# Float32r halves instead of bfloat16 thirds for the score products of an attention kernel, four heads in the four quarters of the matmul array

## The chip, the cores and the metric

One Trainium2 chip, one of its cores. The time is that of one execution on the device, in microseconds (us), from the program's start to its end. The engines named below are TensorE (PE, matmuls; PEld are its weight loads), ScalarE (ACT), VectorE (DVE), GpSimd (POOL) and SyncE (SP, whose queue issues nearly all DMAs).

## What is computed

Eight sequences of 1024 tokens with 128 channels go through four residual blocks: attention with 16 heads of 8 channels, a three-layer FFN with weights of +1 and -1, a windowed attention that keeps the 32 nearest of 64 keys, and the FFN again. The change touches the first block alone:

```python
q = (x @ Wq.T + bq).reshape(b, s, 16, 8) * 8 ** -0.5
k = (x @ Wk.T + bk).reshape(b, s, 16, 8)
v = (x @ Wv.T + bv).reshape(b, s, 16, 8)
probs = softmax(einsum('bqhd,bkhd->bhqk', q, k))
out = einsum('bhqk,bkhd->bqhd', probs, v).reshape(b, s, 128) @ Wo.T + bo
```

x is the layer-normed input. The scores need nearly float32 accuracy, so q and k are each written as a sum of short parts, and the products of the parts are summed in one matmul.

## The kernel before, in words

**Software pipeline over the sequences.** The program runs nine turns. In turn b the attention (side "a") works on sequence b, the head (side "h": norm, projections, splitting q and k) prepares sequence b+1, the sides "o" and "p" carry sequence b-1 through the output projection, the first FFN and the windowed attention, and "q" carries b-2 through the second FFN. Turn 0 has no o, p or q, turn 1 no q, the last turn only the tail. Every engine walks through the same list of stages, which `phases` merges from hand-set spans and weights (lines 119 to 195): each side's stages are given a position, and the list is sorted by it.

**A turn has two phases.** In the first, the *maxima phase*, 64 groups `max` find the maximum of each row of scores. A group is one tile of 128 queries of one pair of heads of a "quad" (four heads). In the second, the *exponential phase*, 128 pairs of score tiles are computed transposed, exponentiated and multiplied by V (`exp`, `pvs`). Into the first phase are merged o, q and most of p; into the second the windowed attention of p and the head h.

**One group of the maxima phase** (lines 835 to 870, 1103 to 1110, 1234 to 1244). For keys k1 (first half) and k2 (second half), max(q.k1, q.k2) = relu(q.(k1 - k2)) + q.k2. PE computes the differences q.(k1 - k2) of both heads into the banks `pair[0]`, two matmuls, and then the far scores q.k2 of both into `pair[1 + g % 2]`, two more. ACT copies the differences with a relu into one of three slots of `pq` (line 1110). DVE subtracts and takes the row maximum, one operation for each head (line 1243). There is one pair of banks for differences (turn 0 has a second), so the differences of group g wait until ACT has taken those of g-1; the far scores of g wait until DVE has taken those of g-2. DVE takes the maxima of g-1 in its stage `max` g. Stage `mrow` closes a quad: the maxima are negated and split into parts too, five small operations, and `mturn` transposes them; SP writes them to DRAM and back into rows of Q (lines 633 to 643), where they meet rows of ones in K, so that the exponential phase gets score minus maximum out of its matmul.

**Rows.** A bfloat16 part holds 8 bits, so q and k have three parts each, and six products of parts are kept: a head takes 6 x 8 = 48 rows of the array and 3 for the maximum. A head starts at row 0 or 64 (`64 * par`), the index `i` picks the other two heads of the quad from another slice of Q and K. The two matmuls of one pair sit in different halves of the rows; the two pairs of one group sit in the same rows.

**Head.** `qk` (lines 721 to 730, 1081 to 1095) and `split` 0 to 4 (lines 731 to 737, 1096 to 1102, 613 to 621) make the parts of q, k and k1 - k2 on ACT (rounding) and POOL (what is left); SP writes the parts to DRAM and `load_quad` (line 524) reads them, spread over the rows, into Q and K: 24 DMAs a quad. Before turn 0 this runs with nothing beside it; line 656 then writes the rows of ones, 16 DMAs.

**Order of POOL.** POOL walks the same list: in the exponential phase it makes the operand `Aop` (line 758) and the mask of the distances (line 765) between the operations of the head. `pass_waits` (line 511) is an increment of a semaphore that nobody waits for.

Of the kernel before, what the change touches and what calls it, by code (L numbers as in the profile page):

```python
# [13 lines left out]
F32 = mybir.dt.float32  # L14
# [15 lines left out]
PARTS = 3  # L30
QPART = (0, 0, 0, 1, 1, 2)
KPART = (0, 1, 2, 0, 1, 0)
QLOAD = ((0, 3, 0), (3, 2, 1), (5, 1, 2))
KLOAD = ((0, 3, 0), (3, 2, 0), (5, 1, 0))
MROW = len(QPART) * HD
KT = T + HALF
# [114 lines left out]
SLOTS_H = [(1.0, [(s, 0)]) for s in ("x", "ln", "lnr", "lnf", "lnn", "lnTa", "qk")] + [(1.0, [("split", i)]) for i in range(5)]  # L151

MAXES = [((g + 0.5) / GROUPS, [("a", "max", (g // QGROUPS, g // NU % 2, g % NU))]) for g in range(GROUPS)]
MROWS = [(((n + 1) * QGROUPS - 0.2) / GROUPS, [("a", "mrow", n)]) for n in range(NQUAD)]

MTURNS = [(((n + 1) * QGROUPS + 2.1) / GROUPS, [("a", "mturn", n)]) for n in range(NQUAD - 1)], [(0.02, [("a", "mturn", NQUAD - 1)])]
# [18 lines left out]
def phases(ahead, behind, twice):  # L175
# [12 lines left out]
    assert not ahead or order.index(("h", "split", 4)) < order.index(("h", "load", 0))  # L188
# [20 lines left out]
HEAD = [("h", s, 0) for s in ("ln", "weights", "lnr", "lnf", "lnn", "lnTa", "qk")] + [("h", "split", i) for i in range(5)]  # L209
# [76 lines left out]
def hybrid_block_kernel(nc, x, Wq, bq, Wk, bk, Wv, bv, Wo, bo, enc_q, enc_v, mn_w1, mn_b1, mn_w2, mn_b2,  # L286
                        base_metric, decoder, heb_U, heb_V, k0, k1, k2, s0, s1, s2, out):
    with ExitStack() as ctx:
# [24 lines left out]
        identb = sb("identb", [P, P], BF16)  # L313
# [37 lines left out]
        pq = sb("pq", [P, PARTS * (T + KT)], BF16)  # L351
        q_parts = pq[:, 0:PARTS * T].rearrange("p (s t) -> p s t", t=T)
        k_parts = pq[:, PARTS * T:PARTS * (T + KT)].rearrange("p (s t) -> p s t", t=KT)
        xna = pq[:, 0:2 * T].bitcast(F32).rearrange("p (u c) -> p u c", c=P)
        Q = sb("Q", [P, NQUAD, 2, T], BF16)

        K = sb("K", [P, NQUAD, 2, KT], BF16)
        Vg = sb("Vg", [P, NU, NH, HD + 1])
        mred = sb("mred", [P, 2, 2, NU])
        nm = sb("nm", [P, 2, 32])  # L360
        mb = sb("mb", [P, PARTS, 32], BF16)
        mT = sb("mT", [PARTS * 32, P], BF16)
# [45 lines left out]
        ones3 = xT[0:PARTS, 0:T // 2].bitcast(BF16)  # L408
# [10 lines left out]
        def place(work, side):  # L419

            late, other = work is LAST and side in ("p", "z"), work is LAST and side in ("q", "z")
            return (xa if late else xr, *((xna, xTa,
                                           Q[:, 0:2].bitcast(F32).rearrange("p n i (f c) -> p (n i f) c", c=HALF),
                                           K[:, 0:2, :, 0:T].bitcast(F32).rearrange("p n i (f c) -> p (n i f) c", c=HALF))
                                          if other else (xn, xT, h1, h2)))
# [16 lines left out]
        steps_m = count("max_steps", 4 * NQUAD)  # L442
# [22 lines left out]
        act_a = count("part_rounded", 6)  # L465
        pool_a = count("part_left", 6)
        kd_a = count("keys_subtracted", 1)
        split_out = [count(f"split_out{part}", 2, 16) for part in range(PARTS)]
        quad_in = [count(f"quad{n}_in", 1, 24 * 16) for n in range(NQUAD)]
# [3 lines left out]
        m_in = count("max_in", NQUAD, 32)  # L473
# [45 lines left out]
        def cut(g):  # L519

            at = 2 * T * (g % RSLOTS)
            return pq[:, at:at + 2 * T].bitcast(F32).rearrange("p (a c) -> p a c", c=HALF)

        def load_quad(eng, n, par, lasts):

            first, parts, part = QLOAD[lasts]
            for i in range(2):
# [993 lines left out]
```

## Time and profile before

| | us |
|---|---|
| median of 3 runs | 3110.93 |
| lowest, highest | 3107.17, 3118.0 |
| the profiled execution | 3113.11 |
| its span, first to last instruction | 3111.4 |
| PE busy | 2513.3 (81%) |
| ACT busy | 2328.1 (75%) |
| DVE busy | 2152.0 (69%) |
| POOL busy | 645.4 (21%) |
| mean granted TensorE clock | 0.907 of 2.4 GHz |

A busy PE is one with a matmul in flight, pipeline latency included; it can be less than full. The maxima phases of turns 0 to 7 begin at 53, 291, 642, 1011, 1376, 1745, 2111 and 2474 us of the span, and the tail fills the last 295 us.

### The profile page before, as it was taken

The page shows a single profiled execution, that of the slowest core. Times are in us where ns is not written, and L with a number is a line of the kernel's source. Part 1 is how long each engine was busy: PE and PEld are TensorE (multiplying, and loading weights), DVE is VectorE, ACT ScalarE, POOL GpSimd, SP SyncE. Part 2 cuts the span into 40 slices and gives each one's busy share as a digit, 9 for nine tenths or more (in the row PEclk, how much of TensorE's full clock was granted, in tenths as well). Part 3 has the DMA queues.
Part 4 walks back from the last instruction along what each step waited for, and adds up shares of the span by engine and source line. Part 5 has one row for each costly group of instructions (what it writes and reads, how often), then busy time and mean ns, then how long its engine had stood idle before and what let it go on. Part 6 is the DMA issues. An engine that isn't in the chain of part 4 may idle for free.

```text
span 3111.4 us, 71098 instructions
## 1 busy us (share of the span) xinstructions
PE 2513.3 (81%) x21555; PEld 1153.9 (37%) x21555; DVE 2152.0 (69%) x10282; ACT 2328.1 (75%) x3241; POOL 645.4 (21%) x820
## 2 busy tenths in 40 slices
PE   4788788888788887888878887888878888887666
PEld 1112343344333443334433343334433344333454
DVE  5801778856786768956689467875679667982695
ACT  4798669967698677976689676995779877895433
POOL 3010114111241113301142012411124111311331
PEclk6599689999899998999999998998989999999888
DMA  2011001100011000100001000110001000000000
GB/s 87 25 45 39 2 9 40 34 18 6 9 47 34 12 13 11 51 28 9 9 33 38 18 9 9 40 34 19 12 2 60 27 8 2 9 2 1 1 8 8
DMA packets 60961, 67.50 MB, mean 22 GB/s; under 512 B 15602, under 2 KB 41908, under 8 KB 60580
## 3 DMA queue, kind: packets, MB, share of 16 engines
q1 hardware_dynamic: 60336, 62.29, 6.2%
q8 instruction: 195, 3.19, 0.4%
q14 instruction: 186, 1.52, 0.2%
q10 hardware_dynamic: 244, 0.49, 0.1%
HBM read 41.95 MB, written 20.71 MB: 20 GB/s over the span
## 4 chain that ended last, share of the span: by engine, by line
PE 38%; ACT 26%; issue 18%; DVE 11%; POOL 4%; SPq 2%; ACTq 0%; DVEq 0%; DMA 0%; POOLq 0%
PE banks L779 36%; ACT PT L1123 12%; DVE pq L1243 3%; POOL Aop L758 3%; ACT pq L1110 2%; PE banks L786 2%; ACT h L1135 2%; DVE xn L1460 1%; DVE h L1463 1%; ACT hparts L1134 1%; ACT Bs L1034 1%; ACT h L1034 1%; ACT xn L1066 1%; ACT h L1182 1%; DVE stat L1215 1%
## 5 line engine op out<-in xcount | busy, mean ns | idle before, releaser
L1123 ACT ACTIVATE PT<-banks 128x1024 f32<-128x1024 f32 x1024 | 999.9, 1035 | 85.2 <-PE banks L779 77.7
L1243 DVE CUSTOM_DVE_ANT_0 pq<-pq,banks 128x512 f32<-128x512 f32 x1024 | 656.7, 685 | 210.9 <-ACT pq L1110 164.5
L1110 ACT ACTIVATE pq<-banks 128x1024 f32<-128x1024 f32 x512 | 522.8, 1022 | 276.0 <-PE banks L779 252.6
L779 PE MATMUL banks<-PT,Vg 128*9 128x512 f32 x4096 | 550.4, 610 | 2.1 <-ACT PT L1123 2.1
L779 PE MATMUL banks<-Q,K 51*128 51x512 bf16 x2048 | 396.9, 394 | 175.8 <-ACT PT L1123 137.5
L779 PE MATMUL banks<-K,Q 48*128 48x512 bf16 x2048 | 376.3, 440 | 114.1 <-ACT pq L1110 63.9
L742 POOL TENSOR_TENSOR hparts<-h,hparts 128x512 fp32r<-128x512 f32 x112 | 140.2, 1272 | 1099.1 <-ACT h L1135 1099.0
L1460 DVE MATCH_REPLACE8 xn<-h,xn 128x96 f32<-128x96 f32 x1536 | 352.4, 243 | 0.0
L779 PE MATMUL banks<-hparts,W 128*128 128x512 f32 x1024 | 314.5, 437 | 37.1 <-ACT h L1135 30.8
L779 PEld LDWEIGHTS banks<-Q,K 51*128 51x128 bf16 x2048 | 109.5, 93 | 616.3 <-issue 584.6
L1463 DVE MAX8 h<-xn 128x8 f32<-128x96 f32 x1536 | 263.4, 244 | 0.3 <-issue 0.2
L765 POOL TENSOR_TENSOR h<-h,outside 128x768 f32<-128x768 f32 x64 | 116.7, 1823 | 643.9 <-DVE h L1443 643.9
L758 POOL TENSOR_SCALAR Aop<-qd,alpha,minus 128x128 f32<-128x128 f32 x512 | 227.1, 459 | 81.9 <-DVEq L1404 70.9
L779 PEld LDWEIGHTS banks<-hparts,W 128*128 128x128 f32 x1024 | 186.1, 200 | 138.8 <-issue 73.8
L779 PEld LDWEIGHTS banks<-K,Q 48*128 48x128 bf16 x2048 | 92.2, 96 | 371.1 <-issue 343.8
L1308 DVE TENSOR_TENSOR Vg<-banks,bvb 128x512 f32<-128x512 f32 x16 | 11.1, 692 | 180.6 <-PE banks L779 180.3
L779 PE MATMUL banks<-B,Aop 128*32 128x96 f32 x4096 | 109.6, 264 | 32.0 <-POOL Aop L758 29.4
L779 PE MATMUL banks<-xT,W 128*128 128x512 f32 x224 | 125.9, 674 | 8.7 <-ACT xT L1034 4.8
L1460 DVE MATCH_VALUE_LOAD xn<-h,xn 128x8 f32 x1536 | 123.0, 80 | 0.3
L779 PE MATMUL banks<-W,h 128*128 128x128 f32 x896 | 115.9, 282 | 6.1 <-ACT h L1034 6.1
L1134 ACT ACTIVATE hparts<-banks,scol 128x512 fp32r<-128x512 f32 x128 | 89.0, 695 | 40.7 <-PE banks L779 40.2
L1460 DVE MATCH_REPLACE8 xn<-h 128x96 f32<-128x96 f32 x512 | 117.3, 241 | 0.0
(204 smaller groups left out, 3423.7 us busy)
## 6 DMA issues: line engine op xcount, KB each, us to landing
scratch_k<-pq SPq DMA_DIRECT2D x24, 384.0 KB, 3.1
K<-scratch_k SPq DMA_DIRECT2D x126, 72.0 KB
qkf<-in_hidden_states SPq DMA_DIRECT2D x16, 512.0 KB, 4.4
scratch_q<-pq SPq DMA_DIRECT2D x24, 256.0 KB, 2.5
Q<-scratch_q SPq DMA_DIRECT2D x126, 48.0 KB
K<-scratch_k SPq DMA_DIRECT2D x126, 48.0 KB
Q<-scratch_q SPq DMA_DIRECT2D x126, 32.0 KB
out<-xr SPq DMA_DIRECT2D x14, 256.0 KB, 2.3
```

The lines of the kernel that those rows point to most:

```text
L742: pool.tensor_tensor(h_lo[:, o, :], h1_[:, o, :], h_hi[:, o, :].bitcast(F32), ALU.subtract).then_inc((low_p if side == "p" else low_q).sem, 1)
L758: ins = pool.tensor_scalar(Aop[:, h, :], qd[:, h // 4, P * n:P * n + P], alpha[:, h:h + 1], minus1[:, h % 4:h % 4 + 1], ALU.mult, ALU.add)
L765: pool.tensor_tensor(d, d, outside[:, :].unsqueeze(1).broadcast_to([P, SH, WW]), ALU.add).then_inc(d_pool.sem, 1)
L779: return pe.matmul(o, l, r, start=start, stop=stop)
L786: ins = pe.transpose(R.bank(k)[:, P * q:P * q + P], src[:, u, :], perm)
L1034: return act.activation(dst, src, func, **kw).then_inc(R.emptied(k), 1)
L1110: act.activation(cut(g), ring_pair if work is TURN0 and g % 2 else pair[0], ACT.Relu).then_inc(diff_out.sem, 1)
L1123: act.activation(PT[:, at:at + 2, :], pair[g % ESLOTS], ACT.Exp, scale=1.0 if i % 8 < 4 else -1.0).then_inc(probs.sem, 1)
L1134: act.activation(h_hi[:, o, :], R.bank(k)[:, :], ACT.Relu, scale=scol[:, 0:1])
L1243: dve.tensor_tensor_reduce(r, r, pair[1 + g % 2][:, par, :], 1.0, -3.0e38, ALU.subtract, ALU.max, mred[:, par, i, qt:qt + 1]).then_inc(max ...
L1460: dve.match_replace(out=Rm[:, h, :], in_to_replace=m8[:, h, :], in_values=src, imm_value=-2 * BIG).then_inc(top8.sem, 1)
L1463: dve.max(out=m8[:, h, :], in_=src).then_inc(top8.sem, 1)
```

## The change

Q and K hold float32r, a 4-byte type of which the matmul uses 12 significant bits. Two parts each and three products of parts make 24 rows a head and 2 for the maximum, so a head fits into 32 rows, and the four heads of a quad take the four quarters (`ROWS * (2 * i + par)`). A group's number now alternates between the two pairs of heads (`i = g % 2`), and PE issues the differences of g and then the far scores of g-1, which lie in the other half of the rows. A new stage `far` issues the last far scores. The head loses the second rounding on ACT and the third part on POOL; `load_quad` issues 16 DMAs a quad, twice the bytes an element. The second part of q, k and k1 - k2 is written to DRAM from where it was computed, so ACT's first write to `xT` in the next turn waits for these DMAs. The transposed maxima come back in four DMAs in place of two, `mrow` has three operations in place of five, and `mrow` and `mturn` stand 0.8 group later.

```diff
-PARTS = 3
-QPART = (0, 0, 0, 1, 1, 2)
-KPART = (0, 1, 2, 0, 1, 0)
...
+PARTS = 2
+QPART = (1, 0, 0)
+KPART = (0, 0, 1)
 MROW = len(QPART) * HD
+ROWS = 32
...
+def group(g):
+
+    return g // QGROUPS, g % 2, g // 2 % NU
+
+
+MAXES = [((g + 0.5) / GROUPS, [("a", "max", group(g))]) for g in range(GROUPS)]
+MAXES.append(((GROUPS - 0.3) / GROUPS, [("a", "far", 0)]))
+MROWS = [((min((n + 1) * QGROUPS + 0.6, GROUPS - 0.2)) / GROUPS, [("a", "mrow", n)]) for n in range(NQUAD)]
+
+MTURNS = [(((n + 1) * QGROUPS + 2.9) / GROUPS, [("a", "mturn", n)]) for n in range(NQUAD - 1)], [(0.02, [("a", "mturn", NQUAD - 1)])]
...
-        Q = sb("Q", [P, NQUAD, 2, T], BF16)
-
-        K = sb("K", [P, NQUAD, 2, KT], BF16)
+        Q = sb("Q", [P, NQUAD, T], F32R)
+        K = sb("K", [P, NQUAD, KT], F32R)
...
+            for t, part, s_ in ((Q, QPART, q_s), (K, KPART, k_s)):
+                first, parts = part.index(lasts), part.count(lasts)
+                for i in range(2):
+                    r = ROWS * (2 * i + par) + HD * first
+                    eng.dma_start(t[r:r + HD * parts, n, :].bitcast(F32),
+                                  s_[lasts:lasts + 1, 4 * n + par + 2 * i].broadcast_to([parts, HD, t.shape[2]])).then_inc(quad_in[n].sem, 16)
...
-                    if stage == "split" and 1 <= n <= 3:
-                        w = n - 1
-                        pool.wait_ge(*act_a.at(b, w + 4))
-                        pool.tensor_tensor(parts_of(w, 2), whole(w), parts_of(w, 1), ALU.subtract).then_inc(pool_a.sem, 1)
...
+            def products(dst, g, keys):
+                n, i, qt = group(g)
+                for par in range(2):
+                    r = ROWS * (2 * i + par)
+                    ins = mm(dst[:, par, :], Q[r:r + MROW, n, P * qt:P * qt + P], K[r:r + MROW, n, keys])
+                return ins
+
+            def far(b, g):
+
+                if g == 1:
+                    pe.wait_ge(*o_out.at(b, 0))
+                    pass_waits(pe)
+                if g >= 2:
+                    pe.wait_ge(*max_out.at(b, g - 1))
+                    pass_waits(pe)
+                products(pair[1 + g % 2], g, slice(HALF, T)).then_inc(far_in.sem, 1)
...
+                        differences = products(diff, g, slice(T, KT))
+                        differences.then_inc(diff_in.sem, 1)
+                        if g >= 1:
+                            far(b, g - 1)
+                    if stage == "far":
+                        far(b, GROUPS - 1)
...
-                            act.wait_ge(*pool_a.at(c, 6))
+                            act.wait_ge(*split_out[PARTS - 1].at(c, 3))
...
-                    if stage == "split" and 1 <= n <= 3:
-                        w = n - 1
-                        act.wait_ge(*pool_a.at(b, w + 1))
-                        act.activation(parts_of(w, 1), whole(w), ACT.Identity).then_inc(act_a.sem, 1)
...
-                        link(dve.tensor_copy(mb[:, 0, :], nm[:, 0, :]))
-                        link(dve.tensor_tensor(nm[:, 1, :], nm[:, 0, :], mb[:, 0, :], ALU.subtract))
-                        link(dve.tensor_copy(mb[:, 1, :], nm[:, 1, :]))
-                        dve.tensor_tensor(mb[:, 2, :], nm[:, 1, :], mb[:, 1, :], ALU.subtract).then_inc(m_red.sem, 1)
+                        link(dve.tensor_copy(mb[:, 0, :], nm[:, :]))
+                        dve.tensor_tensor(mb[:, 1, :], nm[:, :], mb[:, 0, :].bitcast(F32), ALU.subtract).then_inc(m_red.sem, 1)
```

## Rows read from the trace of the kernel before

**Rows 1.** Stretches: maxima phases of turns 1, 4: PE, PEld, DVE, ACT, POOL busy (count), PEclk.

```profile
291.30:452.90 161.60, 127.55 (x625) 63.21 (x623) 113.55 (x371) 101.79 (x152) 15.39 (x17) 0.76 0.03 10
...
1376.20:1555.40 179.20, 148.48 (x778) 80.45 (x775) 120.78 (x401) 121.16 (x189) 25.35 (x25) 0.93 0.04 11
```

**Rows 2.** Stretches: the exponential phase of turn 3, same columns.

```profile
1187.60:1376.20 188.60, 156.09 (x1919) 61.04 (x1917) 148.37 (x885) 168.45 (x216) 53.95 (x72) 0.96 0.10 33
```

**Rows 3.** Chain of waits by line: maxima phase of turn 4, exponential phase of turn 3.

```profile
by line: PE banks L779 41.8%; issue 22.6%; DVE pq L1243 5.4%; ACT h L1135 3.9%; ACT pq L1110 2.9%; PE banks L786 2.7%; ACT xn L1066 2.0%; ACT h L1034 2.0%; ACT hparts L1134 1.8%; POOL Aop L758 1.8%; DVE stat L1215 1.8%; DVE ls L1227 1.4%; D
by line: PE banks L779 34.9%; issue 31.1%; ACT PT L1123 21.1%; POOL Aop L758 4.0%; ACT h L1182 2.4%; ACT Bs L1034 2.0%; ACT h L1179 1.8%; ACT pq L1066 1.5%; ACT oT L1128 1.5%; POOL qkf L730 1.2%; ACT qkf L1034 1.0%; PE banks L786 0.8%; ACT 
```

**Rows 4.** Groups by form, the same two phases: matmuls that the change touches.

```profile
L779 PE MATMUL banks<-K,Q 48*128 48x512 bf16 x255 | 42.6, 399 | 11.9 <-ACT pq L1110 7.5 <-DVE mred L1243 3.5 <-issue 0.2
L779 PE MATMUL banks<-Q,K 51*128 51x512 bf16 x256 | 49.2, 391 | 22.5 <-ACT PT L1123 18.1 <-DVE mred L1243 3.9 <-issue 0.2
```

**Rows 5.** Tiles Q and hparts: weight loads; duration ns min/median/max.

```profile
L779 PEld LDWEIGHTS banks<-K,Q x2048: 92/93/148, 52.1 to 2650.1; 48*128 48x128 bf16 x187
...
L779 PEld LDWEIGHTS banks<-hparts,W x1024: 186/188/391, 359.9 to 3102.7; 128*128 128x128 f32 x171
```

**Rows 6.** Timeline near 1404 us: start, us, engine, what, count.

```profile
1404.08 0.12 PEld L779 LDWEIGHTS banks<-K,Q 48*128 48x128 bf16 x4
...
1404.62 0.50 PE L779 MATMUL banks<-hparts,W 128*128 128x512 f32 x1
```

**Rows 7.** Timeline of PE at 1468 us.

```profile
1468.65 0.61 PE L779 MATMUL banks<-K,Q 48*128 48x512 bf16 x4
1469.18 1.20 PE L779 MATMUL banks<-hparts,W 128*128 128x512 f32 x4
```

**Rows 8.** Timeline of ACT: maxima phase of turn 4, first of 13 short steps, last.

```profile
1404.51 1.03 ACT L1110 ACTIVATE pq<-banks 128x1024 f32<-128x1024 f32 x1 [0.57 <-PE banks L779]
...
1406.17 1.02 ACT L1110 ACTIVATE pq<-banks 128x1024 f32<-128x1024 f32 x1 [0.63 <-PE banks L779]
...
1545.92 1.02 ACT L1110 ACTIVATE pq<-banks 128x1024 f32<-128x1024 f32 x1 [0.57 <-PE banks L779]
```

**Rows 9.** Timeline of ACT, 313 to 347 us, first and last of 18 even steps.

```profile
313.26 1.02 ACT L1110 ACTIVATE pq<-banks 128x1024 f32<-128x1024 f32 x1 [1.65 <-PE banks L779]
...
345.11 1.02 ACT L1110 ACTIVATE pq<-banks 128x1024 f32<-128x1024 f32 x1 [0.85 <-PE banks L779]
```

**Rows 10.** Waits in the maxima phase of turn 4: us in total, times, longest.

```profile
DVE pq L1243 <- ACT pq L1110: 22.6, 24, 2.4
...
PE banks L779 <- DVE mred L1243: 3.5, 5, 1.6
```

**Rows 11.** Timeline of PE, exponential phase: first and last of five Q,K pairs.

```profile
1294.25 0.39 PE L779 MATMUL banks<-Q,K 51*128 51x512 bf16 x2 [0.36 <-ACT PT L1123]
...
1300.41 0.39 PE L779 MATMUL banks<-Q,K 51*128 51x512 bf16 x2
```

**Rows 12.** Waits in the exponential phase of turn 3.

```profile
ACT PT L1123 <- PE banks L779: 9.4, 12, 3.7
```

**Rows 13.** Source lines 1102 and 737: the operations of the third part.

```profile
L1102 ACT ACTIVATE pq<-qkf x16: 1043/1048/1097, 26.0 to 2348.3; 128x1024 bf16<-128x1024 f32 x16
...
L737 POOL TENSOR_TENSOR pq<-qkf,pq x16: 2127/2144/2563, 29.6 to 2349.4; 128x1024 bf16<-128x1024 f32 x16
```

**Rows 14.** Chain of waits before turn 0, and PE's idle time up to 60 us.

```profile
29.64 6.89 POOL pq L737 x3
...
L779 PE MATMUL banks<-K,Q 48*128 48x512 bf16 x26 | 6.5, 614 | 9.9 <-DMA K<-scratch_k 8.0 <-DVE mred L1243 1.9
```

**Rows 15.** Timeline of ACT in turn 0.

```profile
58.01 1.02 ACT L1110 ACTIVATE pq<-banks 128x1024 f32<-128x1024 f32 x1 [0.19 <-DVE mred L1243]
...
61.92 1.02 ACT L1110 ACTIVATE pq<-banks 128x1024 f32<-128x1024 f32 x1 [0.19 <-DVE mred L1243]
...
102.50 0.27 ACT L1034 ACTIVATE mT<-banks 96x128 bf16<-96x128 bf16 x1 [4.60 <-DMA scratch_m<-mT]
```

More of the change, by code:

```diff
@@ L150 @@
 SLOTS_T += [(1.0, [("decd", NU - 1), ("settled", 0)])]
[L151 to L156, printed above, removed]
+SLOTS_H = [(1.0, [(s, 0)]) for s in ("x", "ln", "lnr", "lnf", "lnn", "lnTa", "qk")] + [(1.0, [("split", i)]) for i in range(2)]
+def group(g):
[4 more added lines that the diff above has]
+MTURNS = [(((n + 1) * QGROUPS + 2.9) / GROUPS, [("a", "mturn", n)]) for n in range(NQUAD - 1)], [(0.02, [("a", "mturn", NQUAD - 1)])]
 FIRST_V = [(0.0, [("a", "v", 0)])]
@@ L187, in phases @@
     order = merged(*one) + merged(*two)
-    assert not ahead or order.index(("h", "split", 4)) < order.index(("h", "load", 0))
+    assert not ahead or order.index(("h", "split", 1)) < order.index(("h", "load", 0))
     if twice:
@@ L206, in numbered @@
     return said, use, k
-HEAD = [("h", s, 0) for s in ("ln", "weights", "lnr", "lnf", "lnn", "lnTa", "qk")] + [("h", "split", i) for i in range(5)]
+HEAD = [("h", s, 0) for s in ("ln", "weights", "lnr", "lnf", "lnn", "lnTa", "qk")] + [("h", "split", i) for i in range(2)]
 HEAD += [("h", "load", 0), ("h", "tables", 0)] + [("h", "load", n) for n in range(1, NQUAD)]
@@ L464, in hybrid_block_kernel @@
         xb_a = count("bias_added", 1)
-        act_a = count("part_rounded", 6)
-        pool_a = count("part_left", 6)
+        act_a = count("part_rounded", 3)
+        pool_a = count("part_left", 3)
         kd_a = count("keys_subtracted", 1)
-        split_out = [count(f"split_out{part}", 2, 16) for part in range(PARTS)]
-        quad_in = [count(f"quad{n}_in", 1, 24 * 16) for n in range(NQUAD)]
+        split_out = [count(f"split_out{part}", 3, 16) for part in range(PARTS)]
+        quad_in = [count(f"quad{n}_in", 1, 16 * 16) for n in range(NQUAD)]
         m_red = count("max_split", NQUAD)
@@ L641, in go @@
                         for par in range(2):
-                            r = 64 * par + MROW
-                            sp.dma_start(Q[r:r + PARTS, n, :, :], m_t[:, par]).then_inc(m_in.sem, 16)
+                            for i in range(2):
+                                r = ROWS * (2 * i + par) + MROW
+                                sp.dma_start(Q[r:r + PARTS, n, :].bitcast(F32), m_t[:, par, i]).then_inc(m_in.sem, 16)
                     if stage == "out":
@@ L680, in link @@
                 pool.wait_ge(step, done[0])
-            for t in (ident, flip, identb):
+            for t in (ident, flip):
                 link(pool.memset(t[:, :], 0.0))
```

123 lines of the change are left out of this document (52 added, 71 removed).

## The prediction

> **What bounds the kernel now.** I read the busy shares first: PE 81%, ACT 75%, DVE 69%, so no engine is full and the question is which wait ends last in which phase. The stretches of the two phases answer by phase. In a maxima phase of a full turn PE is busy 148.5 of 179.2 us, ACT and DVE 121 each [rows 1]; in an exponential phase ACT leads with 168.5 of 188.6, PE has 156.1 and DVE 148.4 [rows 2]. The chain of waits says how much of that is on the path: in the maxima phase 41.8% is PE's line 779 and 5.4% DVE's maxima; in the exponential phase 34.9% is PE and 21.1% the exponentials [rows 3]. The matmuls that the change touches are 42.6 us of PE's time in the one phase and 49.2 us in the other [rows 4]. So PE decides in the first phase about half of the time (41.8% of 179.2 is 75 us, of 148.5 busy), and in the second phase PE and ACT take turns.
>
> **What a group costs PE now, and after.** Four score matmuls show 0.61 us from first start to last end, but the next stage starts 0.53 us after them [rows 7]; one matmul of 512 columns shows 0.39 us [rows 11]. The second pair streams behind the first, (0.61 - 0.39) = 0.22 us, because both sit in the same rows. After the change the far scores of g-1 lie in the other rows and can stream beside the differences of g. That takes off 0.22 us.
>
> Against it stands the weight load. A bfloat16 load takes 92 ns, the load of 128 columns in float32r (tile hparts, the same type that Q and K now get) 186 ns [rows 5]. In the bfloat16 case the four loads of a group are all done in 0.12 us, so those in different rows run side by side, and the matmul starts with them; where a float32r matmul follows other work, it shows 0.50 us for the same 512 columns [rows 6], 0.11 us more, which is its load standing open. I take 0.11 us for the first matmul of each burst, nothing for the loads beside it. A group's slot on PE goes from 0.53 to 0.53 - 0.22 + 0.11 = 0.42 us. Bounds for the gain: 0.22 if no load shows, a loss of 0.22 if the four loads go one after another (3 x 0.11 more). The Trainium skill, "TensorE: Matmul & The Clock Gate", section "Weight-path perf modes", speaks against this change: the fast weight load is on for 128 weights of a type that isn't float32, and a plain load takes columns / 1.2 ns, which for 128 columns is an estimate of 107 ns. By that rule the exposed load would be 0.107 us, and the sum below would stay as it is.
>
> **Maxima phases of turns 2 to 7.** (a) PE's half of 64 groups, 32 x 0.11 = -3.5 us a turn. (b) The loop differences, relu on ACT, next differences gets longer, not shorter, since the differences end 0.11 us later. In 13 of the 63 steps of a turn this loop is all there is: they take 1.60 to 1.72 us, against 1.02 us of ACT and 0.39 of PE [rows 8]. 13 x 0.11 = +1.4 us. (c) PE waits 3.5 us a turn for DVE before far scores [rows 10]; far g-1 is now issued a group later and needs the same maxima, so these go: -3.5. (d) DVE pays for it. Its maxima of g-1 could start as soon as ACT was done; now they also wait for the far scores that go out with the differences of g, 0.39 + 0.11 = 0.5 us later. Behind this wait in DVE's queue stand the norm statistics and the turned outputs, for which ACT and PE wait. It costs where DVE's maxima are on the chain: 5.4% of 179 us is 9.7 us, 7 groups, +3.5 us. Together -2.1 us a turn, six turns: **-12.6 us**.
>
> **Turn 1** has 18 steps of even length, 1.87 us each, the first beginning at 313.26 and the last at 345.11 us [rows 9]; they are longer than the 1.60 above because the clock is low (mean granted 0.76 over this phase against 0.93 in turn 4 [rows 1], so much of it at 1.2 GHz). I take the load at up to twice 0.11 there: 18 x 0.2 = +3.6 us, and a small gain elsewhere: **+3 us**.
>
> **Exponential phases.** Here nothing is gained on PE: the two matmuls of a pair already sat in different rows, and each pair now opens with its load. ACT reuses two bank pairs, so 0.11 us is hidden while PE is ahead; it counts where PE is behind. ACT waited for PE before 12 of 128 exponentials, 9.4 us [rows 12]. Such a stretch recurs once for each of eight tiles of p's work: between 1294.25 and 1300.41 us five pairs are issued, the first after a wait for ACT, the other four in a closed row of PE work [rows 11]. 4 x 8 x 0.11 = +3.5 us a turn, seven turns, and 2 us for turn 0, which has no p: **+27 us**. Bounds: 0, and 128 x 0.11 = 14 us a turn.
>
> **Splitting.** ACT loses two operations of 1.05 us and one of half their columns [rows 13], 2.6 us; ACT leads there, so I count all: seven turns, **-18 us**. POOL loses two of 2.14 us and one of half. They stood in POOL's queue ahead of `Aop` and the masks. I count nothing, since `Aop` is on the chain only in part (4.0% [rows 3]); bound -2 us a turn.
>
> **Start and turn 0.** Before turn 0 nothing covers the head: three POOL operations of the third part, 6.89 us, are on the chain, and PE idles 8.0 us for the K load [rows 14]. The last part is ready 6.9 us sooner and SP has four DMAs fewer to issue before it, so the whole wait goes; PE's V products then are next: -8.0. Later ACT stands 4.60 us for the DMA of the first maxima, since SP is still issuing loads [rows 15]; SP now issues 28 fewer. -4.6. DVE sets the pace of turn 0, 3.91 us for three groups [rows 15], and keeps it. **-12.6 us**.
>
> **At nothing.** The bytes of the loads are the same (24 rows of 4 bytes for 48 of 2); the writes to DRAM grow by a third, with 0.10 of the DMA engines busy in that phase [rows 2]. Two more small DMAs a quad on SP, issued 16 steps before their exponentials. ACT's new wait for the DMAs of the second part stands half a phase behind them; without that distance the first FFN would wait. The last far scores go 0.2 group later, and DVE's maxima before them take longer. Two small operations fewer in `mrow`: DVE has idle time.
>
> **Sum.** -12.6 + 3 + 27 - 18 - 12.6 = -13 us. The profiled execution took 3113.1 us, 2.2 above the median, so the median goes from 3110.9 to **3098 us**. A measurement of this kernel can tell about 0.3%, 9.3 us.
>
> **Rivals.**
> 1. *The load stays hidden* (PE loads a quarter while another streams, so no 0.11). For it: the four bfloat16 loads overlap. Against it: the 0.50 us matmul, whose predecessor had the same rows, though. Then +27, +3.6 and 6 x 1.4 us go and the slot gains another 0.11 (32 x 6 x 0.11 = 21 us): 60 us less, **3038 us**. Chance 0.22. The skill's page on TensorE, section "Packing small matmuls", says that a load overlaps matmuls in flight only where the row groups differ; by it this rival would hold for pairs that follow each other directly.
> 2. *DVE becomes late, slower than before.* Place: DVE's wait at line 1243. It waited for ACT's relu 24 times a turn, 22.6 us [rows 10]; each is now a wait for the far scores. If all 24 are on the chain and not 7, 17 x 0.5 x 7 turns = +60 us, **3158 us**; slower by over 0.3% from 6 to 7 more groups a turn on (13 + 9.3 us over 7 turns of 0.5 us). Against it: DVE is busy 121 of 179 us. Chance 0.20.
> 3. *The loads of the four quarters go one after another*: slot 0.74 us, pairs another 0.11 late, about +120 us (0.32 x 32 x 6 = 61, 0.11 x 32 x 7 = 25, the loops the rest), **3218 us**. The 0.12 us for four loads speak against it. Chance 0.06.
> 4. *The clock.* PE streams for half the time in the maxima phase; granted clock was 0.93 there in turn 4 but 0.76 in turn 1, which has less beside the scores [rows 1]. If a quarter of the groups fall to 1.2 GHz, 16 x (1.87 - 1.60) x 6 = +26 us, **3124 us**. Chance 0.08.
>
> The forecast has 0.44, with 3075 to 3125 as its own range. Faster: half of the forecast's case and rival 1, 0.44; same: 0.19; slower: the rest, 0.37. The range reaches to rival 1 and well into rival 2: 3035 to 3150.
>
> **What would show it.** In the new profile: K,Q loads of 186 ns and four matmuls that start together and span 0.50 us; 13 short steps at 1.70 us; no waits for line 1243's result before far scores, DVE waits at 1243 on PE in place of ACT; PE's first score at 44 us instead of 52; no 4.6 us stall; exponential phases 1 us longer. Wrong if K,Q loads still show 92 ns, or if the exponential phases shrink by more than the 2.6 us of ACT.

## The result, and the profile after

Slower. The kernel after takes 3287.3 us (median of four, 3276.4 to 3294.0) beside 3112.7 for the kernel before (four runs): a ratio of 1.056, 95% interval 1.052 to 1.060. Forecast were 3098 us, with 3035 to 3150 as range, so the time lies 137 us outside of it. The profiled execution of after took 3294.0 us, its span is 3292.3.

From the page of after, part 1 and the clock's row of part 2:

```profile
PE 2741.7 (83%) x21555; PEld 1372.9 (42%) x21555; DVE 2080.1 (63%) x10218; ACT 2321.2 (71%) x3217; POOL 602.5 (18%) x795
...
PEclk6598769899898987799888997888988898789888
```

PE is busy 228 us longer, DVE and POOL are busy less. The mean granted clock fell from 0.907 to 0.855. The stretches say where the time lies. After: maxima phase of turn 1, exponential phase of turn 3, maxima phase of turn 4, and the last stretch (exponential phase of turn 7 and the tail); the sums are those of the exponential phases of turns 1 to 6 and of the maxima phases of turns 2 to 7 (columns as in [rows 1]).

```profile
296.80:468.20 171.40, 124.73 (x625) 73.08 (x625) 110.03 (x366) 101.99 (x151) 15.47 (x17) 0.73 0.03 10
...
1246.50:1461.50 215.00, 190.50 (x1918) 80.11 (x1917) 142.38 (x881) 167.63 (x214) 48.61 (x69) 0.83 0.10 34
...
1461.50:1647.00 185.50, 155.21 (x777) 93.00 (x777) 116.88 (x396) 121.95 (x189) 25.45 (x25) 0.88 0.03 10
...
2809.60:3292.30 482.70, 365.04 (x3667) 204.18 (x3665) 316.87 (x1870) 273.25 (x411) 116.53 (x162) 0.86 0.02 5
...
sum 1237.60, PE 1102.37 PEld 461.58 DVE 853.65 ACT 1004.36 POOL 291.09; mean PE 183.73 PEld 76.93 DVE 142.28 ACT 167.39 POOL 48.52
...
sum 1103.80, PE 919.54 PEld 551.58 DVE 700.70 ACT 729.49 POOL 152.85; mean PE 153.26 PEld 91.93 DVE 116.78 ACT 121.58 POOL 25.47
```

The same stretches of before that [rows 1, 2] do not have, last stretch and the two sums:

```profile
2650.60:3111.40 460.80, 340.86 (x3667) 190.70 (x3665) 317.35 (x1873) 272.07 (x411) 116.11 (x162) 0.89 0.02 5
...
sum 1129.20, PE 939.79 PEld 362.60 DVE 892.23 ACT 1011.37 POOL 323.73; mean PE 156.63 PEld 60.43 DVE 148.70 ACT 168.56 POOL 53.96
...
sum 1068.50, PE 899.51 PEld 487.79 DVE 723.00 ACT 726.57 POOL 152.16; mean PE 149.92 PEld 81.30 DVE 120.50 ACT 121.09 POOL 25.36
```

So of the 180.9 us by which the span grew, 108.4 lie in the six exponential phases (1237.6 - 1129.2), 35.3 in the six maxima phases, 21.9 in the last stretch, 9.8 in the maxima phase of turn 1, and 5.5 in the rest. The large loss is where the order of the matmuls was not changed. In the exponential phase of turn 3, the slowest of the six, the granted clock is 0.83 against 0.96 [rows 2] (0.85 to 0.88 in the other five, against 0.95 to 0.97), ACT waits for PE 33.2 us before its exponentials against 9.4 [rows 12], and matmuls that the change doesn't touch got longer too. Groups by form in that phase, of after and then of before:

```profile
L784 PE MATMUL banks<-PT,Vg 128*9 128x512 f32 x512 | 79.4, 697 | 0.2 <-ACT PT L1137 0.2
L784 PE MATMUL banks<-Q,K 26*128 26x512 f32 x256 | 65.3, 557 | 16.4 <-ACT PT L1137 12.9 <-DVE mred L1257 3.0 <-issue 0.2
```

```profile
L779 PE MATMUL banks<-PT,Vg 128*9 128x512 f32 x512 | 67.8, 602 | 0.2 <-ACT PT L1123 0.2
```

The products with V use no load from Q or K, so the load cannot be their reason. It is the clock. In this phase the matmuls on Q and K take, as shortest, median and longest in ns:

```profile
L784 PE MATMUL banks<-Q,K x256: 461/497/791, 1249.9 to 1450.8; 26*128 26x512 f32 x128
```

791 is what one takes at 1.2 GHz with its load: in the stretch from 1256.5 to 1266.5 us, where the granted clock is 0.50 throughout, the median is 788. Stretches of 10 us within the phase (same columns) show both levels beside each other, the last line one of before:

```profile
1336.50:1346.50 10.00, 8.41 (x118) 3.49 (x118) 9.83 (x74) 10.00 (x14) 4.71 (x9) 1.00 0.01 2
1346.50:1356.50 10.00, 10.00 (x49) 3.99 (x49) 4.32 (x26) 5.87 (x9) 0.00 (x0) 0.55 0.01 2
1356.50:1366.50 10.00, 9.76 (x182) 5.19 (x174) 8.44 (x53) 8.50 (x11) 5.30 (x9) 0.94 0.03 9
1366.50:1376.50 10.00, 9.42 (x38) 3.15 (x34) 6.52 (x38) 6.54 (x9) 0.00 (x0) 0.57 0.38 117
...
1247.60:1257.60 10.00, 6.99 (x111) 2.66 (x109) 9.83 (x69) 10.00 (x14) 7.96 (x11) 1.00 0.38 141
```

From 1346.5 to 1356.5 us PE has a matmul in flight all the time and is still granted 0.55, nearly all of it at 1.2 GHz; before the fall it was busy 8.41 of 10 us. In the phase of before no stretch of 10 us from 1217.6 to 1367.6 us is below 1.00, not even behind one with 6.99 us of busy PE. The Trainium skill, "TensorE: Matmul & The Clock Gate", Part 1, says that the gate follows how busy the PE has been recently. The busy shares of these stretches do not explain the fall: it came behind 8.41 here and not behind 6.99 there. So the first question was what else the clock follows.

Timeline of after in the maxima phase of turn 4, two bursts of four score matmuls and their loads (start, us, engine, what, count), then the ACT steps of the loop:

```profile
1500.57 0.51 PE L784 MATMUL banks<-K,Q 24*128 24x512 f32 x4
1502.31 0.70 PE L784 MATMUL banks<-K,Q 24*128 24x512 f32 x4
```

```profile
1500.56 0.19 PEld L784 LDWEIGHTS banks<-K,Q 24*128 24x128 f32 x4
1502.31 0.39 PEld L784 LDWEIGHTS banks<-K,Q 24*128 24x128 f32 x4 [0.36 <-issue]
```

```profile
1509.86 1.02 ACT L1124 ACTIVATE pq<-banks 128x1024 f32<-128x1024 f32 x1 [1.39 <-PE banks L784]
1511.57 1.02 ACT L1124 ACTIVATE pq<-banks 128x1024 f32<-128x1024 f32 x1 [0.69 <-PE banks L784]
```

The step of 1.71 us is as forecast (1.70). A burst has two forms: 0.51 us with the four loads side by side in 0.19, as forecast, and 0.70 us with the loads of one pair after those of the other, 0.39. The second form is longer than the 0.61 of the bfloat16 burst [rows 7], and it is the more frequent one: of the 63 bursts of four in this phase, 22 take 0.50 to 0.54 us and 41 take 0.62 or more (some of these at 1.2 GHz).

### The profile page after: what moved, and what is told of

Its sections match the earlier page's. It is cut to its first block, busy times and chain, and to the rows that moved or that the text cites. A ratio compares the mean times of both kernels' runs of the same rounds, so it can differ in the third digit from the quotient of the medians.

```text
span 3292.3 us, 70740 instructions
## 1 busy us (share of the span) xinstructions
PE 2741.7 (83%) x21555; PEld 1372.9 (42%) x21555; DVE 2080.1 (63%) x10218; ACT 2321.2 (71%) x3217; POOL 602.5 (18%) x795
## 4 chain that ended last, share of the span: by engine, by line
PE 46%; ACT 23%; issue 16%; DVE 9%; POOL 3%; SPq 2%; DMA 1%; ACTq 0%; DVEq 0%; POOLq 0%
PE banks L784 43%; ACT PT L1137 11%; DVE pq L1257 3%; ACT pq L1124 2%; POOL Aop L763 2%; PE banks L791 1%; SPq L540 1%; DVE xn L1472 1%; ACT xn L1084 1%; ACT h L1149 1%; DVE stat L1229 1%; ACT h L1052 1%; ACT Bs L1052 1%; DVE h L1475 1%; ACT hparts L1148 1%
## 5 line engine op out<-in xcount | busy, mean ns | idle before, releaser
L784 PE MATMUL banks<-Q,K 26*128 26x512 f32 x2048 | 512.7, 538 | 134.4 <-ACT PT L1137 107.2
L784 PE MATMUL banks<-PT,Vg 128*9 128x512 f32 x4096 | 608.5, 670 | 2.2 <-ACT PT L1137 2.2
L784 PE MATMUL banks<-K,Q 24*128 24x512 f32 x2048 | 378.5, 564 | 105.6 <-ACT pq L1124 80.7
L784 PEld LDWEIGHTS banks<-Q,K 26*128 26x128 f32 x2048 | 207.7, 198 | 606.8 <-issue 583.3
L784 PEld LDWEIGHTS banks<-K,Q 24*128 24x128 f32 x2048 | 176.0, 214 | 328.8 <-issue 302.4
L784 PE MATMUL banks<-B,Aop 128*32 128x96 f32 x4096 | 123.4, 285 | 44.4 <-POOL Aop L763 26.0
L784 PE MATMUL banks<-xT,W 128*128 128x512 f32 x224 | 134.1, 716 | 18.5 <-DVE xr L1381 13.9
L1448 DVE TENSOR_TENSOR h<-banks,an 128x384 f32<-128x384 f32 x128 | 71.0, 557 | 123.8 <-PE banks L784 120.6
L784 PEld LDWEIGHTS banks<-B,Aop 128*32 128x32 f32 x4096 | 108.7, 130 | 70.1 <-issue 38.2
L784 PEld LDWEIGHTS banks<-PT,Vg 128*9 128x9 f32 x4096 | 61.6, 89 | 149.5 <-issue 134.7
```

Of the source, the lines that this page charges most:

```text
L784: return pe.matmul(o, l, r, start=start, stop=stop)
L1448: dve.tensor_tensor(D[:, n % 2, 4 * f:4 * f + 4, :], R.bank(k)[:, 0:4 * WW].rearrange("p (j w) -> p j w", w=WW), cast(an[:, n, SH + 4 * f: ...
```

## The theories and the first four experiments

**Theory A**: the clock is granted by how much of the array works, and a matmul on 24 or 26 rows counts for less than one on 48 or 51. **Theory B**: float32r costs, by its exposed load or by its type. The twelve runs below are all compared with the kernel before on the same chip (medians 3113 to 3117 us; the ratio leaves out the profiled execution). Sums of phases are of the one profiled execution of each kernel. In before and in two kernels whose exponential phases do the same work on the same rows (zeros in 24 rows, few rows in the maxima phase alone) these phases sum to 1129.2, 1130.4 and 1127.7 us, so two or three microseconds there say nothing.

**Few rows in the kernel before.**

```diff
-rows_ = slice(64 * par, 64 * par + MROW + PARTS)
+rows_ = slice(64 * par + 32, 64 * par + MROW + PARTS)
-scale=1.0 if i % 8 < 4 else -1.0
+scale=1.0e-3 if i % 8 < 4 else -1.0e-3
```

> The kernel before (bfloat16, heads in halves), but the score matmuls of the exponential phase read only the last 19 of a head's 51 rows (rows 32 to 50 and 96 to 114), and the exponential's scale is 0.001 of what it was, so that nothing overflows: it leaves out most of the score products. Instructions, columns, waits and weight loads of 92 ns stay as they are. Theory A (the clock is granted by how much of the array works, so fewer rows for the same time cost clock): mean granted clock falls from 0.907 to about 0.86, the exponential phases grow from 189 to about 200 us, time 3200 to 3290 us. Theory B (the loss comes from float32r: its exposed load, or its type): clock 0.907, time 3113 within 0.3%.

Measured: 3252.4 us, ratio 1.043 (1.038 to 1.048), clock 0.853. Exponential phase of turn 3, maxima phase of turn 4, sum of the exponential phases of turns 1 to 6:

```profile
1236.70:1439.50 202.80, 172.06 (x1919) 64.51 (x1917) 147.32 (x884) 169.47 (x216) 53.98 (x72) 0.87 0.10 31
1439.50:1616.30 176.80, 149.22 (x777) 81.17 (x775) 120.66 (x401) 121.16 (x189) 25.36 (x25) 0.92 0.04 11
...
sum 1249.50, PE 1076.55 PEld 400.87 DVE 885.81 ACT 1016.62 POOL 323.85; mean PE 179.42 PEld 66.81 DVE 147.63 ACT 169.44 POOL 53.98
```

With the type, the loads and the order of before, and only the rows fewer, the exponential phases take 120 us more and lie at the clock of after; the maxima phases, not edited, stay as they were (1060.8 against 1068.5). A load that stays at 91 ns cannot do that, so theory A holds here, unless the scale or the values did it; the zeros below settle that.

**More rows in the kernel after.**

```diff
-r = ROWS * (2 * j + par)
-rows_ = slice(r, r + MROW + PARTS)
+rows_ = slice(64 * par, 64 * par + 64)
...
+dve.memset(Q[:, :, :].bitcast(F32), 0.0)
+dve.memset(K[:, :, :].bitcast(F32), 0.0)
```

> The changed kernel (float32r, heads in quarters), but each score matmul of the exponential phase reads 64 rows, a half of the array, for two heads at once (rows between the heads are zero): it computes sums of two heads' scores in place of each. Count, columns, loads (181 ns) and concurrency as before. Theory A: the clock comes back to about 0.90, exponential phases to 190 to 194 us, time 3110 to 3170 us. Theory B: clock 0.857, time 3287 within 0.5%.

Measured: 3209.9 us, ratio 1.031 (1.029 to 1.033), clock 0.888, so 77 us come back, although zeroing Q and K holds the first scores back by 7 us. Exponential phase of turn 3 and the sum:

```profile
1224.10:1417.90 193.80, 169.25 (x1918) 73.42 (x1917) 142.26 (x881) 166.40 (x213) 48.51 (x69) 0.95 0.11 36
...
sum 1157.30, PE 1014.21 PEld 438.07 DVE 855.30 ACT 998.78 POOL 290.72; mean PE 169.03 PEld 73.01 DVE 142.55 ACT 166.46 POOL 48.45
```

64 rows in place of 26 give 80 of the 108 us back, and the clock of these phases, between 0.83 and 0.88 in after, is 0.95. The whole time stays above what theory A alone forecast (3110 to 3170).

**The upper halves read as bfloat16.**

```diff
+def high(ap):
+    return ap.bitcast(BF16)[:, 1::2]
...
-ins = mm(dst[:, par, :], Q[r:r + MROW, n, P * qt:P * qt + P], K[r:r + MROW, n, keys])
+ins = mm(dst[:, par, :], high(Q[r:r + MROW, n, P * qt:P * qt + P]), high(K[r:r + MROW, n, keys]))
```

(the exponential's matmuls alike)

> The changed kernel, but every score matmul reads the upper two bytes of Q and K as bfloat16: it leaves out the lower bits of each part, so scores are less exact. Rows (24 and 26 in quarters), order and columns stay; only the type and the weight load (92 ns for 181) change. Theory A: the clock stays low (0.85 to 0.87); the time falls only by the exposed loads, 3220 to 3270 us. Theory B: clock 0.90 or more, time 3050 to 3110 us.

Measured: 3198.0 us, ratio 1.027 (1.024 to 1.031), clock 0.861: 89 us less than after. Sum of the exponential phases:

```profile
sum 1185.80, PE 1008.39 PEld 385.66 DVE 855.29 ACT 997.70 POOL 289.83; mean PE 168.06 PEld 64.28 DVE 142.55 ACT 166.28 POOL 48.30
```

The load went from 181 to 92 ns, the exponential phases fell by 51.8 us, the maxima phases from 1103.8 to 1084.3. The mean clock hardly moved (0.855 to 0.861), but in the exponential phases it rose: 0.87 to 0.91, against 0.83 to 0.88. The time is below the range of theory A (3220 to 3270) and above that of B (3050 to 3110): each names a part of the loss.

**The old order of the maxima groups.** `group(g)` counts as before, and PE issues the far scores of g right behind the differences of g, in the same rows.

```diff
-    return g // QGROUPS, g % 2, g // 2 % NU
+    return g // QGROUPS, g // NU % 2, g % NU
...
-                        if g >= 1:
-                            far(b, g - 1)
+                        far(b, g)
```

> The changed kernel with the order of before: the far scores of g right behind the differences of g, in the same rows, groups numbered as before. It takes back the overlap of the two pairs and the maxima's wait for PE. If the overlap is worth what the sum said (0.22 us for half of 64 groups, 7 turns, less DVE's lag and PE's waits, which cancel): 25 to 50 us slower than 3287. If DVE's lag weighs more: faster than 3287, down to 3250. If Theory A holds for the maxima phase too, PE streams longer there and the clock in these phases goes from 0.88 to about 0.90, which takes back part of the loss.

Measured: 3424.4 us, ratio 1.099 (1.096 to 1.101), clock 0.814. Maxima phase of turn 4, sum of six, and a burst:

```profile
1527.60:1723.40 195.80, 171.70 (x777) 100.76 (x775) 120.18 (x395) 122.10 (x190) 25.40 (x25) 0.83 0.03 10
...
sum 1200.90, PE 1065.42 PEld 619.92 DVE 714.70 ACT 734.23 POOL 152.66; mean PE 177.57 PEld 103.32 DVE 119.12 ACT 122.37 POOL 25.44
```

```profile
1562.36 0.73 PE L784 MATMUL banks<-K,Q 24*128 24x512 f32 x4
```

The new order is worth 137 us to float32r in quarters, where 25 to 50 were expected. The two profiled executions lie 152 us apart, 97 of them in the maxima phases. At 2.4 GHz most bursts take 0.73 here, against 0.51 or 0.70. The expectation also had the clock of these phases rise, since PE streams longer; it fell: 0.71 to 0.86, against 0.86 to 0.91. The two pairs of a group now stream one after the other through the same rows of the same two quarters, so fewer rows work at a time, which fits theory A, but no run separates this from the longer bursts. The exponential phases grew by 33 us with not a line of theirs edited; why is not explained.

## What of the rows counts, the order alone, and both costs together

**Zeros in 24 of the 51 rows.** The kernel before; Q's first rows aren't loaded and hold zeros.

```diff
-for i in range(2):
+for i in range(2 if lasts else 0):
...
+dve.memset(Q[:, :, :, :], 0.0)
```

> Leaves out: the kernel before, where the first 24 of the 51 rows that each half holds of Q are not loaded but hold zeros, and the exponential is scaled by 0.001; its score products therefore lack their first terms. The same rows are addressed by every matmul as before, at the same instants. This asks what it is about rows that the clock answers to. If the clock falls because fewer rows are addressed (theory A in its narrow form), nothing changes: 3113 us, mean granted clock 0.907, exponential phases of 188 us. If it falls because fewer rows carry live numbers (theory A, data form), 24 of 51 rows without live products lower the clock about half as far as the kernel that reads 19 of 51 did: some 3180 to 3250 us, clock 0.86 to 0.88. If the scale of 0.001 or other values alone moved the clock in the earlier experiment, that shows here as well, with both theories. Some 15 us may go for four fewer small DMAs at each turn.

Measured: 3107.0 us, ratio 0.9968 (0.9953 to 0.9983), clock 0.908; exponential phases of turns 1 to 6:

```profile
sum 1130.40, PE 939.59 PEld 362.13 DVE 885.22 ACT 1011.42 POOL 325.15; mean PE 156.60 PEld 60.36 DVE 147.54 ACT 168.57 POOL 54.19
```

Zeros cost nothing that shows (1130.4 against 1129.2), nor does the scale of the exponential, which this kernel has as well. What counts is how many rows a matmul addresses, not what they hold. The 0.3% fits the DMAs left out.

**Few rows in the maxima phase alone.**

```diff
-rows_ = slice(64 * par, 64 * par + MROW)
+rows_ = slice(64 * par + 32, 64 * par + MROW)
```

(and the exponential's scale of 0.001, as in the first experiment)

> Leaves out: the kernel before, where the score matmuls for the maxima read 16 of their 48 rows, and the exponential is scaled by 0.001; the matmuls for the exponentials keep 51 rows. Theory A (the granted clock follows how many rows of the array work): the maxima phases of turns 2 to 7, 1068 us together at a clock near 0.92, fall to 0.85 to 0.88 and grow by 10 to 20 us each, 3180 to 3230 us; the exponential phases stay at 188 us and 0.95. Theory B (only float32r costs, and what the earlier run of few rows showed belongs to the exponential phase alone): 3113 us.

Measured: 3222.0 us, ratio 1.037 (1.030 to 1.044), clock 0.874 in the profiled execution. The four executions spread from 3188.4 (the profiled one) to 3253.2 us; the shortest is still 2.3% above before. Maxima phases of turns 2 and 4 and their sum:

```profile
645.70:839.60 193.90, 169.40 (x777) 89.11 (x775) 118.82 (x401) 121.62 (x189) 25.48 (x25) 0.81 0.04 11
...
1400.20:1593.90 193.70, 170.21 (x777) 89.13 (x775) 118.45 (x401) 121.91 (x190) 25.48 (x25) 0.80 0.03 10
...
sum 1138.80, PE 992.02 PEld 524.07 DVE 714.91 ACT 729.51 POOL 152.86; mean PE 165.34 PEld 87.34 DVE 119.15 ACT 121.59 POOL 25.48
```

In turn 4 the clock falls from 0.93 to 0.80 (in the six phases it is 0.80 to 0.88, against 0.90 to 0.93). The six phases are 70 us longer, and the exponential phases, not edited, keep their 0.95 to 0.97 (1127.7 us).

**The new order in the kernel before**, with `far` and the later `mrow`, `mturn` as in after; bfloat16 and halves stay.

```diff
-for dst, keys in ((diff, slice(T, KT)), (pair[1 + g % 2], slice(HALF, T))):
...
+products(diff, g, slice(T, KT)).then_inc(diff_in.sem, 1)
+if g >= 1:
+    far(b, g - 1)
```

> Leaves nothing out. The kernel before with its bfloat16 thirds in two halves, and only the order changed: the differences of g stand ahead of the far scores of g-1. By the prediction's terms (c) and (d), without the overlap: the 3.5 us a turn of PE's waits for the maxima go, DVE's maxima come 0.39 us later on 7 groups on the chain, 2.7 us a turn: 3108 us, no difference. By rival 2 (all 24 waits of the vector engine on the chain): 17 x 0.39 x 7 = 46 us more, 3157 us. By the large gain that the order had with float32r in quarters (137 us): if that gain was the overlap of different rows, nothing of it shows here; if part of it was that PE no longer stands with a closed queue behind the vector engine, the maxima phases fall by 5 to 20 us each and this beats the kernel before, 3000 to 3080 us.

Measured: 3150.9 us, ratio 1.011 (1.009 to 1.014), clock 0.900. Sum of the maxima phases of turns 2 to 7; waits in that of turn 4:

```profile
sum 1091.40, PE 890.87 PEld 484.83 DVE 707.59 ACT 727.70 POOL 152.85; mean PE 148.48 PEld 80.80 DVE 117.93 ACT 121.28 POOL 25.47
```

```profile
DVE pq L1255 <- PE banks L780: 47.0, 44, 5.6
...
PE banks L780 <- ACT pq L1122: 8.4, 8, 3.2
```

The order alone costs 22.9 us in six phases, 3.8 a turn: DVE now waits 44 times for PE in place of 24 times for ACT [rows 10]. Of the whole loss (1.1%, 34 us), 7 more lie in the exponential phases (1135.8). The expectation had 3108 us by the prediction's terms and 3157 by rival 2; the 3150.9 lie nearer to the rival.

**Both costs of after taken away**: 64 rows in the exponential phase and the upper halves as bfloat16 everywhere (the second and the third edit together).

> Leaves out: the kernel after, where the exponential's score matmuls read 64 rows (the quarters of two heads and the gaps between, zeroed), and every score matmul reads the upper halves as bfloat16 (the weight load of 92 ns): neither more exact parts nor separate heads. This takes away both suspected costs together. Rows gave 3287 - 3210 = 77 us back, the type 89 us. If the two are separate (theory A for the rows, B for the load), both go: 3120 to 3150 us, exponential phases at 186 to 190 us and a clock of 0.95, maxima phases still at 0.87 since they stay at 24 rows. If the type acted through the clock as well (one cause counted twice), less goes: 3170 us and more. What remains above 3113 is the maxima phase at fewer rows.

Measured: 3142.1 us, ratio 1.008 (1.006 to 1.011), clock 0.890. Sums of the maxima and of the exponential phases:

```profile
sum 1088.70, PE 889.66 PEld 505.87 DVE 701.67 ACT 727.18 POOL 152.94; mean PE 148.28 PEld 84.31 DVE 116.95 ACT 121.20 POOL 25.49
```

```profile
sum 1130.00, PE 947.27 PEld 364.28 DVE 856.56 ACT 997.77 POOL 291.13; mean PE 157.88 PEld 60.71 DVE 142.76 ACT 166.29 POOL 48.52
```

Of the 174.6 us of loss 145 go (3287.3 - 3142.1), 21 less than the 77 and 89 of the single edits add up to: the two costs overlap. The exponential phases show it. Rows first, then type: 1237.6 to 1157.3 is the rows (80.3), 1157.3 to 1130.0 the type (27.3). Type first: 1237.6 to 1185.8 is the type (51.8), 1185.8 to 1130.0 the rows (55.8). Some 24 us are thus due to either. Together the two take away all but 0.8 us of what these phases lost, and their clock is back at 0.95 to 0.96. One reason for the overlap is in the matmuls: float32r in place of bfloat16 lengthens one by 0.10 us at 2.4 GHz (497 against 394 ns, medians) and by some 0.18 us at 1.2 GHz (788 against the 605 that is the longest in bfloat16), so the type costs more where the rows have lowered the clock.

## Does it count rows or groups of 32, and is there anything to gain

Up to here fewer rows always came with smaller tiles of the array as well (32 rows in place of 64). The next kernel keeps the tile.

**All 32 rows of a quarter** (26 before), six of them zeros.

```diff
-rows_ = slice(r, r + MROW + PARTS)
+rows_ = slice(r, r + ROWS)
...
+for n in range(NQUAD):
+    dve.memset(Q[:, n, :].bitcast(F32), 0.0).then_inc(gaps, 1)
+    dve.memset(K[:, n, :].bitcast(F32), 0.0).then_inc(gaps, 1)
```

> Leaves nothing out. The kernel after, where the exponential's score matmuls read all 32 rows of a quarter, of which six hold zeros, in place of 26. If the clock answers to the rows that a matmul addresses, one by one, 26 to 32 rows is a quarter of the way to the 64 that gave 77 us back: 3287 - 15 to 25 = 3262 to 3272 us, exponential phases at a clock of 0.88 to 0.90. If it answers to which row groups of 32 a matmul occupies, nothing changes, 3287 us, since 26 rows occupy the whole group already. Some 2 us of delay at the start are in either.

Measured: 3261.9 us, ratio 1.048 (1.046 to 1.051), clock 0.866: 25 us less than after, as rows counted one by one forecast (3262 to 3272); by groups of 32 nothing should have changed. Sum of the exponential phases:

```profile
sum 1190.90, PE 1049.12 PEld 447.19 DVE 853.80 ACT 1001.24 POOL 289.99; mean PE 174.85 PEld 74.53 DVE 142.30 ACT 166.87 POOL 48.33
```

Six rows of zeros in the same tiles give 47 of the 80 us of 38 rows back in these phases, at a clock of 0.88 to 0.95. That is more than the quarter that was expected: that the net came out as forecast is in part luck, since the maxima phases of this execution were 13 us longer and the first scores came 6.5 us later. So rows within a group of 32 count, but not in proportion. Whether the tile's size has a share of its own besides is open.

**All 64 rows in the kernel before**, first in the exponential's matmuls, then also in those of the differences (Q and K zeroed at the start as above; K's rows 48 to 63 hold zeros in the columns of the differences).

```diff
-rows_ = slice(64 * par, 64 * par + MROW + PARTS)
+rows_ = slice(64 * par, 64 * par + 64)
...
-rows_ = slice(64 * par, 64 * par + MROW)
+rows_ = slice(64 * par, 64 * par + (64 if dst is diff else MROW))
```

> Leaves nothing out. The kernel before, where the exponential's score matmuls read all 64 rows of their half, of which 13 hold zeros, in place of 51. If the clock answers to rows addressed: the exponential phases, at 0.95 granted with 51 rows and 0.83 to 0.88 with 19, go to 0.96 to 0.98 and shorten by 1 to 3 us each: 3113 - 7 to 20 us = 3093 to 3106 us. If it answers to groups of 32 (both halves are occupied already): 3113 us to 3116 us, the start being 2 us later.

> Leaves nothing out. The kernel before with 64 rows both in the exponential's score matmuls and in the matmuls of the differences (zeros in the keys' rows 48 to 63, so nothing is added). If the clock answers to rows addressed: the maxima phases, 0.92 granted with 48 rows and 0.80 to 0.88 with 16, gain a fifth of that for half of their matmuls: clock 0.93, 1 to 3 us each, 3080 to 3100 us together with the exponential phases, faster than both kernels. By groups of 32: 3113 to 3116 us.

Measured: 3114.7 us, ratio 1.0009 (1.0000 to 1.0019), clock 0.911; and 3111.4 us, 0.9988 (0.9977 to 0.9998), clock 0.912. Both miss what rows counted one by one forecast; the first lies where groups of 32 had it. But their maxima phase of turn 0 starts at 58 us and not at 52 to 53: the zeros, 9 us of DVE, stood ahead of the first norm. The last kernel writes them in DVE's wait for a table, which ended at 26.5 us in the trace of before:

```diff
 if stage == "tables":
+    for m in range(NQUAD):
+        dve.memset(Q[:, m, :, :], 0.0).then_inc(gaps, 1)
+        dve.memset(K[:, m, :, :], 0.0).then_inc(gaps, 1)
     dve.wait_ge(loaded, LOADS * 16)
```

> Leaves nothing out. The same kernel with 64 rows in the exponential's matmuls and in those of the differences, with the zeros written while the vector engine waits for a table (9.7 to 26.5 us in the trace of before), in place of ahead of its first work, where they held the first scores back by 6 us. If rows addressed beyond 51 and 48 still help the clock a little (theory A), the two kernels with zeros at the start gave 3115 and 3111 us with a start 6 us later, and this one comes to 3103 to 3108 us, faster than before by 0.15 to 0.35%. If their clock of 0.911 and 0.912 against 0.907 was chance, 3113 us.

Measured: 3106.3 us (eight runs) beside 3114.7 (twelve), ratio 0.9973 (0.9963 to 0.9984), clock 0.917. Exponential phases:

```profile
sum 1122.50, PE 933.64 PEld 362.11 DVE 888.83 ACT 1010.10 POOL 323.71; mean PE 155.61 PEld 60.35 DVE 148.14 ACT 168.35 POOL 53.95
```

It computes all that before does and is faster than both kernels, if by 0.27% only. The exponential phases are 6.7 us shorter in this execution, 2.6 and 4.3 in those of the two kernels above; the maxima phases are not (1068.9 against 1068.5), though half of their matmuls now have 64 rows. Where the granted clock is 0.95 already, more rows have little left to give.

## Why the prediction was wrong, step by step

**The step that failed** is the clock. The prediction has it as a rival for the maxima phase alone (chance 0.08, +26 us) and says of the exponential phases only "each pair now opens with its load". It read the clock from how long PE streams, since 0.93 and 0.76 [rows 1] went with more and less work beside the scores. That half the rows in the same streaming time would lower it was nowhere in the sum. The runs put it at 56 to 80 us in six exponential phases, as the type is taken away first or after it, plus part of the last stretch, whose clock went from 0.89 to 0.86. The prediction's signs of being wrong did not catch this: the loads show 181 ns, and the exponential phases did not shrink; they grew by 18 us each where 1 was forecast.

**The load.** The mechanism was right, the size nearly so: at a clock of 0.95 on both sides the load costs 27.3 / 6 = 4.6 us per exponential phase, and "4 x 8 x 0.11 = +3.5 us a turn" was forecast. The rows of 186 and 0.50 us [rows 5, 6] were the right ones. In a maxima phase it costs (1108.9 - 1088.7) / 6 = 3.4 us; 1108.9 is the sum of the kernel with more rows. At the lower clock it is dearer: in the whole the type is worth 89 us with 26 rows and 68 with 64 (3209.9 - 3142.1).

**The splitting, "-18 us".** Not seen. ACT is busy 2.3 us less in a phase (166.3 against 168.6 in the mean), yet with rows and type taken out of the account the six phases are 0.8 us longer than before, not 15.6 shorter. "ACT leads there, so I count all" was wrong: to lead in busy time is not to be on the chain with every operation; 21.1% [rows 3] was the measure at hand.

**Maxima phases.** (a) forecast bursts of 0.50 us; they take that or 0.70, when the loads of the second pair come after those of the first. That is rival 3's mechanism for up to 41 of 63 bursts. It is not the type's: in the kernel with the upper halves read as bfloat16, 24 of 62 bursts take 0.40 to 0.44 us and the others 0.53 or more. (b) holds: 1.71 us steps. (c) and (d) were to cancel; the order alone costs 3.8 us a turn here, and 34 us in the whole. (c) brought little: with the order alone PE still waits 2.1 us for DVE and 8.4 for ACT (3.5 and 7.5 before), and its idle time before score matmuls goes from 11.9 to 11.2 us, in after to 9.2. So (d) costs more than the 2.7 us that 0.39 us for 7 groups gives. The mechanism of rival 2 exists: 34 of the 46 us that it had for this kernel in the whole, though in the maxima phases alone 3.8 us a turn, where the rival has 17 x 0.39 = 6.6 beyond the terms. With the load taken away, but still at 24 rows, the phases are 20 us longer than before (1088.7), at a clock of 0.86 to 0.90. The order (22.9) and the load (20.2) add up to 43 us where 35.3 were lost; what of the rest is the gain of the overlap and what the cost of the clock, no run separates.

**Turn 1**: +3 forecast, +9.8 measured, at a clock of 0.73 against 0.76.

**Start and turn 0, "-12.6 us".** They are 5.5 us longer. The first score starts at 52.7 us and not at 44 (before 52.1). The maxima phase of turn 0 did get shorter, 83.7 us against 89.0 at a clock of 0.50 in both, but its exponential phase takes 159.5 against 149.4, at 0.89 against 0.94, so the clock and the load count there too. Views of after: waits up to 60 us, SP's issues before the first score, and ACT's waits in turn 0:

```profile
PE banks L784 <- DMA K<-scratch_k: 12.3, 1, 12.3
```

```profile
42.98 5.29 SPq L540 DMA_DIRECT2D K<-scratch_k  x2
```

```profile
ACT mT L1052 <- DMA scratch_m<-mT: 5.9, 1, 5.9
```

The arithmetic was shorter, but the wait was not for it: PE stands 12.3 us for K in place of 8.0, and the first maxima's DMA keeps ACT 5.9 us in place of 4.60 [rows 14, 15]. "The bytes of the loads are the same" hides that the DMAs are fewer and larger (up to 64 KB for Q and 96 for K, in place of 48 and 72); one pair of issues on SP took 5.29 us, where the others take 0.7 to 1.7. Why that one stood was not tried.

## What to carry to other kernels

Fewer rows for the same work is not free on this array. A matmul that streams as many columns through fewer rows takes the same time at a given clock (512 columns in bfloat16: 385 ns as median with 19 rows, 386 with 51 and with 64), and the clock is granted lower (0.82 to 0.87 in the exponential phases with 19 rows, 0.95 to 0.97 with 51). When an edit narrows matmuls, compare the granted clock by phase before anything else, and look whether matmuls that it doesn't touch got longer. Where the zeros can be written in an idle stretch, matmuls that include rows of zeros can be the cheaper ones (25 us of 3287 for six rows, 8 us of 3115 where the clock was high already). What a type costs must be counted at both clock levels, 0.10 and some 0.18 us a matmul here, and two costs that act through the same clock should be taken away one by one and together before either gets a price.

## What the hardware showed that was not expected

Rows addressed, not numbers in them, move the clock, here as a mean over the whole execution: 51 rows 0.907, 19 rows in the exponential phases 0.853, 24 of 51 rows zero 0.908. A float32r load of 128 columns takes 181 ns with 24 rows and 183 with 64, against 91 to 93 in bfloat16, and float32r streams 512 columns in the time that bfloat16 does: a matmul shows 497 ns with its load exposed, 383 as shortest, against a median of 386 in bfloat16. At 1.2 GHz the load takes 283 ns. Loads of different quarters run side by side only in part of the bursts, four in 0.19 us or in 0.39.
